# A fused decoder layer with routed experts: another order of VectorE's work in the tile step, and a later copy of a batch's rows on GpSimd

## What is computed

```python
x = layernorm(x + self_attention(x))          # 16 heads of 64, causal
x = layernorm(x + cross_attention(x, ctx))    # 16 heads of 16, with a mask and biases
x = layernorm(x + moe(x))
# moe: two groups of 32 experts each; in each group a token goes to its two best experts
#   scores = softmax(x2 @ router); weights, chosen = top_k(scores, 2)
#   ys = (silu(x @ wg[e]) * (x @ wu[e])) @ wd[e], hidden size 128
#   out_g[token] += weight * ys
# out = (2 * out_0 + 2 * out_1) / 4
```

## Time and profile before

| | us |
|---|---|
| median of 3 runs | 4889.1 (4886.68 to 4891.63) |
| the profiled execution | 4894.84 |
| its span, first to last instruction | 4893.1 |
| mean granted TensorE clock | 0.992 |

### The profile page before, as it was taken

One profiled execution on the slowest core, in us unless ns is written; L12 is line 12 of the kernel. 1 busy time (PEld: TensorE's weight loads), 2 busy tenths in 40 slices (PEclk: granted clock), 3 DMA queues, 4 the chain that ended last, 5 costly groups with the idle time before them and its releaser, 6 DMA issues. The chain is left out here.

```text
span 4893.1 us, 133371 instructions
## 1 busy us (share of the span) xinstructions
PE 4755.2 (97%) x38848; PEld 3976.5 (81%) x38848; DVE 3782.2 (77%) x18828; ACT 3412.7 (70%) x13380; POOL 2712.7 (55%) x3750
## 2 busy tenths in 40 slices
PE   7999999999999999999999999999995999999998
PEld 6888888888888888888888888888874766676665
DVE  4888888888888888888888888888883455547777
ACT  5788888878878888887887888788783444444443
POOL 3455555555555555555555555555554555556666
PEclk9999999999999999999999999999997999999999
DMA  4121111112112111211211211121125799878888
GB/s 137 62 69 61 58 65 64 57 60 69 58 58 67 62 58 64 65 58 57 67 62 57 67 64 58 61 67 58 58 78 162 255 299 298 273 246 270 273 273 255
DMA packets 477157, 556.18 MB, mean 114 GB/s; under 512 B 55602, under 2 KB 407860, under 8 KB 475956
## 3 DMA queue, kind: packets, MB, share of 16 engines
q1 hardware_dynamic: 350516, 300.08, 19.9%
q0 software_dynamic: 52224, 146.87, 8.0%
q10 hardware_dynamic: 73728, 100.70, 6.8%
HBM read 270.08 MB, written 277.35 MB: 112 GB/s over the span
## 5 line engine op out<-in xcount | busy, mean ns | idle before, releaser
L527 POOL TENSOR_TENSOR yTl<-yT,yTh 128x256 fp32r<-128x256 f32 x512 | 381.7, 745 | 910.7 <-DVE yTh L979 907.6
L756 ACT ACTIVATE prob<-prob,negmax 128x128 f32<-128x128 f32 x2048 | 799.0, 395 | 102.5 <-DVE negmax L827 98.3
L1155 POOL DMA_INDIRECT y_d<-y,to x576 | 593.2, 1030 | 464.6 <-DVE y L1290 447.8
L756 ACT ACTIVATE xprob<-xprob,xnegmax 128x128 f32<-128x128 f32 x2048 | 792.9, 392 | 1.6 <-DVE xnegmax L827 1.6
L1208 PE MATMUL bank<-moe,xgT 128*128 x2304 | 594.6, 381 | 0.0
L589 POOL DMA_INDIRECT xs_d<-xrow,place x512 | 515.9, 1008 | 128.1 <-issue 128.1
L1290 DVE COPY y<-bank 128x256 f32<-128x256 f32 x576 | 244.5, 424 | 407.4 <-PE bank L1224 290.0
L827 DVE CUSTOM_DVE_ANT_0 prob<-bank,causal 128x128 f32<-128x128 f32 x2048 | 471.7, 286 | 34.0 <-PE bank L695 20.9
L774 ACT COPY probT<-bank 128x512 f32<-128x512 f32 x512 | 300.0, 586 | 248.0 <-PE bank L705 181.1
L827 DVE CUSTOM_DVE_ANT_0 xprob<-bank,xmask 128x128 f32<-128x128 f32 x2048 | 470.5, 286 | 1.2 <-remote 1.2
L837 DVE TENSOR_TENSOR prob<-prob,inv 128x512 f32<-128x512 f32 x512 | 438.9, 857 | 20.2
(11 more groups left out here) (180 smaller groups left out, 14188.3 us busy)
## 6 DMA issues: line engine op xcount, KB each, us to landing
xg<-xs_d SPq DMA_DIRECT2D x576, 136.0 KB
xs_d<-blank SPq DMA_DIRECT2D x248, 272.0 KB
rows<-y_d ACTq DMA_DIRECT2D x256, 256.0 KB
xT_s<-xT SPq DMA_DIRECT2D x128, 128.0 KB
x<-x SPq DMA_DIRECT2D x128, 128.0 KB, 2.0
cT<-cT SPq DMA_DIRECT2D x128, 128.0 KB
x_d<-x SPq DMA_DIRECT2D x128, 128.0 KB, 2.0
sums<-x_d ACTq DMA_DIRECT2D x128, 128.0 KB
```

The source lines that it names most:

```text
L527: nc.gpsimd.tensor_tensor(yT_p[1][:, c, :], yT[:, c, :], yT_p[0][:, c, :].bitcast(F32), ALU.subtract).then_inc(y_split, 1)
L756: last = nc.scalar.activation(dst[:, h, :], dst[:, h, :], ACT.Exp, bias=src_bias[:, h:h + 1], scale=-1.0, accum_out=acc[:, h:h + 1])
L1155: nc.gpsimd.indirect_dma_start(y_d[:, :], bass.IndirectOffsetOnAxis(ap=to[:, m % NTO:m % NTO + 1].bitcast(U32), axis=0), y_s[q][:, :], Non ...
```

## The change

VectorE's `to` and `h` of tile n-1 become the first work of its step in the second part; the first sum, the copy of `y` and the second sum follow. On GpSimd `token_rows` moves from group 1 (ahead of `open_blocks`) to group 3, behind the scatters. The tiles of `xg` get 258 numbers a row instead of 272, and only these are loaded.

```diff
@@ GpSimd's iteration, first part
-                            if s == 1 and t.live(4):
-                                token_rows(t.item(4))
                             if s == 2 and t.live(4):
                                 open_blocks(t.item(4))
                             if t.live(5):
                                 scatter(t.item(5), s)
+                            if s == 3 and t.live(4):
+                                token_rows(t.item(4))
@@ second part
-            xg_s = [sb(f"xg{q}", [P, ROW]) for q in range(NX)]
+            xg_s = [sb(f"xg{q}", [P, D + 2]) for q in range(NX)]
-                            sp.dma_start(xg_s[q][:, :], xs_d[g][(n - g * TILES) * P:(n - g * TILES + 1) * P, :]).then_inc(xg_in[q], 16)
+                            sp.dma_start(xg_s[q][:, :], xs_d[g][(n - g * TILES) * P:(n - g * TILES + 1) * P, 0:D + 2]).then_inc(xg_in[q], 16)
@@ VectorE's iteration, second part
                     def iteration(t, n):
+                        if t.live(1):
+                            q, m = t.slot(1), t.item(1)
+                            dve.wait_ge(gate_in, m + 1)
+                            wait(dve, ht_made, t.item(2))
+                            v.tensor_tensor(to[:, m % NTO:m % NTO + 1], xg_s[m % NX][:, CODE:CODE + 1], spare_no[:, m % SPARE:m % SPARE + 1],
+                                            ALU.max).then_inc(to_made, 1)
+                            v.tensor_tensor(h_s[q % 2][:, :], gate_s[q % 2][:, :], GB[q % 2][:, HID:2 * HID], ALU.mult).then_inc(h_in, 1)
                         now = combined(n - COMBINE)
...
                             v.scalar_tensor_tensor(s[:, :], rows[:, k % NR, 1, :], weight_of(g, b, 1), s[:, :], ALU.mult, ALU.add).then_inc(sum_ready, 1)
-                        if t.live(1):
-                            q, m = t.slot(1), t.item(1)
-                            dve.wait_ge(gate_in, m + 1)
-                            wait(dve, ht_made, t.item(2))
-                            v.tensor_tensor(to[:, m % NTO:m % NTO + 1], xg_s[m % NX][:, CODE:CODE + 1], spare_no[:, m % SPARE:m % SPARE + 1],
-                                            ALU.max).then_inc(to_made, 1)
-                            v.tensor_tensor(h_s[q % 2][:, :], gate_s[q % 2][:, :], GB[q % 2][:, HID:2 * HID], ALU.mult).then_inc(h_in, 1)
```

## The result

The changed kernel takes 4910.65 us in the median of six runs (4907.15 to 4914.77), the kernel before 4890.6 (4886.68 to 4893.33, six runs): ratio 1.0041, interval 1.0028 to 1.0054. It is slower by 20 us where a gain of 36 was forecast.

The account below looks back on a forecast made before the run. TensorE bounds the kernel, held in the expert tiles by VectorE's `h`. Profiled 4894.8 - 130 (tile-step order) + 0 (short rows) + 94 (moved copy) = 4858.8, less 5.7 to the median: 4853 us; range 4755 to 4900.

Parts of the forecast that it names:

- What bounds the kernel: TensorE: in attention and routing any hold-up is paid in full; in the expert tiles `h` decides, unhindered step 1.68 us.
- Part 1: Expert tile step, `to` and `h` first on VectorE: wait for `h` goes, 1.70 us a step, -130 us.
- rival 2: TensorE's table-word register load in the tile step is not hidden: 1.78 us a step, 4892 us, no change; chance 0.15.
- rival 3: Expert tiles: the four `y` buffers run out, a 6.9 us landing sets the step to 1.90: 4961 us; chance 0.10.
- Part 2: Expert tiles, `xg` rows of 258 instead of 272 numbers: 7 KB less a tile, hidden anyway, 0 us.
- Part 3: GpSimd's row copy moved to the end of group 3 blocks VectorE's scaling: 0.75 us for 126 batches, +94 us.
- the copy will start at 2019.7: End of group 3: the moved copy starts as the fourth slot's scatter ends (2019.69), beside VectorE's L837 at 2019.72.
- the forecast price: End of group 3, copy just ahead of L837: 0.77 us lost a batch; 0.75 taken over both orders.
- its other case: End of group 3, L837 first: the copy takes its turn next and holds L844, 0.68 us lost a batch.
- The upper bound, 108: Most that the moved copy was to cost in the first part: 0.86 us x 126 batches = 108 us.
- Rival 1: End of group 3: the moved copy misses VectorE's scalings, only the tile-step gain counts, 4759 us; chance 0.12.

Follow-up runs that it names:

- part 1 alone: The kernel before with one edit, `to` and `h` first in VectorE's tile step: 4758.06 us, ratio 0.973.
- the doubled load: The kernel after with the copy back in group 1, table-word load issued twice in TensorE's queue; the second load was not in the program that ran: 4777.51 us.
- the difference early: The kernel after with VectorE's subtraction L943 moved ahead of the two index searches: 4888.58 us, ratio 0.9998.

## Why the prediction was wrong, step by step

**What bounds the kernel.** Right. Any idle time of TensorE in the first part was paid in full, and in the second part the end that decided was `h`. The floor of a tile step was put at 1.68 us; in the kernel after it is lower, 1.62 to 1.63 for one step after the other, with `h`'s transpose 0.87 behind the start of the matmuls. So not all of the 1.68 was TensorE's own work, as the prediction had it:

```profile
3961.40 1.03 PE L1208 MATMUL bank<-moe,xgT 128*128 x4
3962.27 0.27 PE L1219 MATMUL bank<-ident,h 128*128 128x128 f32 x1
...
3963.03 1.03 PE L1208 MATMUL bank<-moe,xgT 128*128 x4
```

**Part 1.** Right. 575 x 1.70 = 978 us was forecast without the stretches in which expert weights are loaded, 985 with them; 978.2 was measured, and part 1 alone gives 132 us against 130. The size is partly luck. The mean step of 1.70 was put together as a floor of 1.68 and 0.02 left of the register load; it came out of a floor of 1.63 (937 us for 575 steps), some 17 us for the register loads, and 24 us in longer steps for which the sum had only the 7 of the weight loads. The new wait at the head of VectorE's step did no harm. Two lines of the waits of the kernel after, from 3909 to 4888 us, VectorE for the gate and TensorE for `h`; the second was 86 us in the kernel before:

```profile
DVE to L1283 <- ACT gate L1244: 225.9, 335, 3.9
...
PEld bank L1219 <- DVE h L1285: 12.0, 30, 1.1
```

**The register load** (rival 2). It didn't come. Of the load's 0.31 us most is hidden: in the kernel after the step with it takes 1.71 us in the median against 1.63, and the step behind it 1.66, together 0.12 us once in four steps. The 0.38 that the rival needed is not there. How far ahead TensorE's queue runs, 0.36 us or another length, no run shows, as the doubled load was not in the program.

**The `y` buffers** (rival 3). They are waited for, by VectorE, but with room:

```profile
DVE y L1297 <- DMA y_d<-y,to: 30.1, 50, 1.6
```

50 copies of 576 stood for 0.6 us on average, at 304 GB/s where 312 were worked out, and the part still came out at 978. The price of this rival (22 us saved instead of 137) is far off.

**Part 2.** Right: 0, measured 1.0004.

**Part 3.** This is the step that failed, by its size: +94 forecast with bounds of 0 and 108, +148 measured in the first part, and that alone turned a gain of 36 us into a loss of 20. The reading that the end of group 3 has no slack was right, that the copy blocks VectorE was right, and so was when the block ends (0.14 before the copy's end there, 0.12 here). What failed is the sentence "the copy will start at 2019.7". It took the copy's recorded start for the start of the block. In the earlier trace rows the scatter runs from 2018.73 to 2019.69, and I looked only at what VectorE starts behind that. But VectorE starts L943, with two inputs in SBUF, in that same place, 0.48 us before the scatter's end:

```profile
2019.21 0.14 DVE L943 TENSOR_TENSOR below<-top 128x2 f32<-128x2 f32 x1
```

In the kernel before nothing free to start stood behind the scatter, and L943 took 0.14 us. With the copy there, the block began while the scatter ran and met L943 first: 1.42 held instead of 0.86, and 1.25 us in each of 117 batches instead of 0.75 in 126. Taking the two small instructions away brought back the forecast price (0.79; L837 was held for 1.00 there instead of 0.86, but started 0.11 earlier against the scatter's end), making the copy wait brought back its other case (0.56 against 0.68), and the copy ahead of the scatters brought back all of it.

The upper bound, 108, failed for the same reason: it was the longest block that the trace had shown, not the longest that it allowed. The bound from the rows would have been the copy's 1.03 us plus the part of the scatter in which VectorE has an instruction to start, 0.48: (1.03 - 0.14 + 0.48 - 0.09) x 126 = 161 us. The 0.48 is partly hindsight: the trace of the kernel before says where VectorE starts, but shows no block during a scatter. With that bound the range would have reached to 4853 - 94 + 161 = 4920, and the 4911 lie inside.

The Trainium skill (SBUF — State Buffer, "Who interferes with whom") names instructions that take part: a cast can, a tensor_tensor with two SBUF inputs does against a GpSimd instruction that reads SBUF, and one with at most one SBUF input outside the two-port modes does not. The trace agrees: the cast and the difference were held (1.38 and 1.56 us), and L944, with an input in PSUM, was not (0.20). The reciprocal was not either (0.17). The page says that issue order decides who blocks. Recorded starts don't give that order here: the difference started 0.49 us ahead of the copy by the record, L837 with nothing else in its way 0.08 ahead, and both were held; with the waiting copy the same scaling (L839) started 0.01 ahead and was not.

**Rival 1**, that the copy misses, gave 4759, the time of the kernels with the copy in group 1 or ahead of the scatters (4757, 4760). Its price was right. Behind the scatters its case does occur, but in four batches of the steady part only, those with the late copy (iteration 28.54).

## What to carry to other kernels

When a GpSimd instruction that reads SBUF is moved, look at everything that VectorE starts while the GpSimd instruction ahead of it runs (here from 0.66 us ahead of the copy's recorded start), down to the smallest: a 128x2 difference with two SBUF inputs, or a 128x4 cast, stands for the whole copy if it comes first, and all that is queued behind it stands too. Where such a copy must lie beside a path without slack, split it in pieces, or give it a semaphore to wait for, so that VectorE's next instruction is not caught. And bound a collision by the longest that the rows allow (the instruction's own length and the overlap with the one before it), not by the longest that they happen to show.

## What the runs showed of the hardware

- A GpSimd copy of 128x1024, free to start behind an indirect DMA, holds a VectorE instruction that starts up to 0.66 us before the copy's recorded start, until 0.12 before its end (L943, 1.56 us for 0.14 us of work; the cast with the difference early, 1.38 for 0.15). One that starts 0.67 us or more before it was free. The reciprocal (128x4, SBUF to SBUF) was free 0.29 us before it. With the copy waiting for a semaphore there was no such hold in 128 batches (143 ns at most).
- A write of constants between the two doesn't break the hold (1.69 us), though it reads nothing. Ahead of a copy of 128x512 the difference was let go 0.14 us before the copy's recorded start, ahead of four copies of 128x256 0.36 before the first one's, and ahead of one of 128x1024 not before its end. What decides that is open.
- It goes both ways: where VectorE's scaling and the copy started within 0.01 us of each other, the copy took 1.58 us for 1.04 us of work.
- A register load in TensorE's queue (305 ns) cost about 0.12 us a time in steps of 1.63 us.
- The same instructions gave a second part of 978.3 us in one profiled run and of 993.0 in another, on another chip, at a granted clock of 0.992 and 0.991.
